# Two transformer blocks with 16 small heads: a head's stack in half of the partitions, restacked in three chunks, no clearing

## What is computed

```python
ada = silu(c) @ W_ada + b_ada            # six vectors of 144: shift, scale, gate, twice
h = layernorm(x) * (1 + scale) + shift
q, k, v = split(h @ W_qkv + b_qkv)       # 16 heads of 9 channels
p = softmax(q @ k.T / 3)                 # block 1: keys after the query are masked out
x = x + gate * ((p @ v) @ W_proj + b_proj)
h = layernorm(x) * (1 + scale2) + shift2
x = x + gate2 * (act(h @ W_fc1 + b_fc1) @ W_fc2 + b_fc2)
```

## Time and profile before

| | us |
|---|---|
| three runs, median (lowest to highest) | 379.49 (379.43 to 381.12) |
| profiled execution, first to last instruction | 382.2 |
| TensorE busy (2020 matmul instructions) | 305.8 |
| VectorE busy | 260.8 |
| ScalarE busy | 195.1 |
| POOL busy | 72.8 |

### The profile page before, as it was taken

The page is one execution under the profiler, slowest core; times in us unless marked ns, Lnnn a source line. Parts: engine busy times, 40 slices in busy tenths (PEclk is TensorE's granted clock), DMA queues, the critical chain, the costliest instruction groups (busy, mean ns, idle before and its releaser), DMA issues.

```text
span 382.2 us, 5927 instructions
## 1 busy us (share of the span) xinstructions
PE 305.8 (80%) x2020; PEld 165.7 (43%) x2020; DVE 260.8 (68%) x575; ACT 195.1 (51%) x414; POOL 72.8 (19%) x157
## 2 busy tenths in 40 slices
PE   2044399697999999889993879999953999999567
PEld 2023282122334363445341545565431565647366
DVE  6999589674858798996851667879633668831363
ACT  4037310274573755894781127745613456894352
POOL 5934500010102615501100010110100011010000
PEclk9999585588989999999997968999968799999969
DMA  6402645420000000000044100000451000000000
GB/s 173 116 0 79 143 92 157 103 72 17 1 2 2 0 4 1 2 1 3 1 121 100 60 7 0 3 1 13 128 96 53 3 1 3 3 1 17 16 2 31
DMA packets 11285, 15.57 MB, mean 41 GB/s; under 512 B 1774, under 2 KB 9909, under 8 KB 10824
## 3 DMA queue, kind: packets, MB, share of 16 engines
q1 hardware_dynamic: 10744, 15.00, 14.9%
q0 software_dynamic: 512, 0.20, 0.2%
HBM read 10.67 MB, written 4.13 MB: 39 GB/s over the span
## 4 chain that ended last, share of the span: by engine, by line
PE 53%; DVE 17%; DMA 14%; issue 6%; ACT 5%; SPq 4%; POOL 1%; DVEq 0%; ACTq 0%; POOLq 0%
PE PB L1147 11%; PE OB L1167 10%; DMA KS<-qk_parts 10%; PE PB L1129 9%; PE PB L1209 5%; DVE hn L968 4%; DMA QS<-mT 3%; SPq L668 3%; DVE negm L1014 3%; PE PB L1104 3%; DVE parts L998 2%; DVE rest L995 2%; PE PB L1174 2%; PE PB L1064 2%; PE PB L1150 1%
## 5 line engine op out<-in xcount | busy, mean ns | idle before, releaser
L1014 DVE TENSOR_REDUCE negm<-PB 128x1 f32<-128x512 f32 (+3 forms) x256 | 136.3, 583 | 62.4 <-PE PB L1131 39.2
L841 ACT ACTIVATE probs<-PB 128x512 f32<-128x512 f32 (+3 forms) x256 | 116.4, 521 | 80.2 <-PE PB L1150 47.0
L1129 PE MATMUL PB<-KS,QS 96*128 96x512 bf16 (+3 forms) x256 | 87.2, 387 | 21.1 <-DMA KS<-qk_parts 20.3
L1147 PE MATMUL PB<-QS,KS 96*128 96x512 bf16 (+3 forms) x256 | 81.4, 360 | 8.5 <-DMA QS<-mT 6.9
L1167 PE MATMUL OB<-probs,V 128*10 128x512 f32 (+3 forms) x512 | 59.7, 538 | 0.9 <-ACT probs L841 0.6
L1129 PEld LDWEIGHTS PB<-KS,QS 96*128 96x128 bf16 x256 | 26.2, 105 | 65.5 <-issue 42.0
L1147 PEld LDWEIGHTS PB<-QS,KS 96*128 96x128 bf16 x256 | 25.0, 101 | 52.9 <-issue 34.1
L768 POOL CAST msp<-negm 128x16 bf16<-128x16 f32 x16 | 4.3, 266 | 161.6 <-DVE negm L1014 161.6
L1104 PE MATMUL PB<-ident,hn 128*16 128x128 f32 (+1 forms) x64 | 12.1, 336 | 22.7 <-DVE hn L968 22.7
L1131 PE MATMUL PB<-mask_qk,identb 128*128 128x128 bf16 x128 | 29.4, 244 | 0.0
L1150 PE MATMUL PB<-mask_kq,identb 128*128 128x128 bf16 x128 | 27.0, 226 | 0.0
(11 more groups left out here) (135 smaller groups left out, 453.6 us busy)
## 6 DMA issues: line engine op xcount, KB each, us to landing
qk_parts<-parts SPq DMA_DIRECT2D x8, 384.0 KB, 2.5
QS<-qk_parts SPq DMA_DIRECT2D x4, 324.0 KB
KS<-qk_parts SPq DMA_DIRECT2D x4, 324.0 KB
QS<-qk_parts SPq DMA_DIRECT2D x8, 108.0 KB
KS<-qk_parts SPq DMA_DIRECT2D x8, 108.0 KB
QS<-qk_parts SPq DMA_DIRECT2D x4, 216.0 KB
KS<-qk_parts SPq DMA_DIRECT2D x4, 216.0 KB
X<-in_x SPq DMA_DIRECT2D x2, 288.0 KB, 3.2
```

The costliest lines, as they stand in the source:

```text
L841: nc.scalar.activation(probs[:, kt % 2, j, q0:T], bank_of(item)[:, q0:T], ACT.Exp, scale=SCALE).then_inc(bank_free[BANK[item]], 1)
L1014: nc.vector.tensor_reduce(negm[:, g % 2, qt, j:j + 1], bank[:, 0:keys_of(g // (B * NG), qt)], AX.X, ALU.max, negate=True).then_inc(bank_fr ...
L1129: ins = nc.tensor.matmul(o[:, 0:w], q, KS[b][0:KROWS, h + j, 0:w], start=True, stop=(l == 0))
L1147: ins = nc.tensor.matmul(bank[:, q0:T], KS[b][0:KROWS, h + j, kt * P:(kt + 1) * P], QS[b][0:KROWS, h + j, q0:T], start=True, stop=(l == 0))
```

## The change

- A head's stack takes 57 rows (KROWS = MROW + 3) and no cleared rows. Even heads lie at partitions 0 to 56, odd heads at 64 to 120; `QS` and `KS` are 128 x 8 x 512. Products of an even and of an odd head thus use different row tiles of TensorE.
- Units of a group run tile by tile with the four heads inside (`UNITS`), so parity alternates. In block 1 the two masks of a pair are issued together behind its second product.
- `qk` is cut in three chunks of heads (0 to 6, 7 to 13, 14 and 15), each with its queries and keys. SP writes each chunk's six slots to DRAM with six DMAs and reads them back with four (queries and keys, even and odd heads). Each chunk has its semaphores. The memsets and the copy that cleared stacks are gone; ones are sent once per batch and parity.
- `hT`: the last 16 channels are modulated on VectorE before the transpose (`hr`, five operations), stacked there, transposed as 96 columns. The fp32r split of the first 128 channels is gone: `qk` and `fc1` are one float32 product over 128 channels and one fp32r product of 96 rows. `wsplit` shrinks to stacking the last rows.
- `acol` computes the modulation of the last 16 channels for all partitions (wide products). `proj`'s residual product has 17 rows.
- Block 1's MLP: ScalarE writes tanh only, VectorE's gate reads x from the bank; the factors 0.5 are moved to the gate weights.
- Batch 0's x and the first qkv weights are loaded on ScalarE's queue. The maxima's parts go by two DMAs of POOL instead of one. Weights no longer share memory with MLP buffers.
- The planner has new costs and priorities (HASTE for batch 0's head 2000 instead of 20000, HOLD for shift 1 instead of 2).

```diff
-KROWS = 96
+CHUNKS = [(0, 7), (7, 14), (14, H)]
+STRIP = P // 2
+SLOTS = 6
+MROW = SLOTS * D
+KROWS = MROW + 3
...
+UNITS = [(t, j) for t in range(NT) for j in range(HG)]
...
+        def strip(h, n):
+            return slice(STRIP * (h % 2), STRIP * (h % 2) + n)
...
+                if kind == "parts":
+                    sp.wait_ge(parts_ready, QKN[("qk", l, b, i)])
+                    n = width(i) // 2
+                    for w, runs in enumerate((((0, 3, 1, 0), (0, 2, 1, 3), (0, 1, 1, 5)),
+                                              ((0, 1, 3, 0), (1, 1, 2, 3), (2, 1, 1, 5)))):
+                        for s, many, times, slot in runs:
+                            src = parts[w * n:(w + 1) * n, i, s:s + many, :]
+                            if times > 1:
+                                src = src.to_broadcast([n, times, T])
+                            dst = scratch[l][b][i][w, slot:slot + many * times].rearrange("s d h t -> (d h) s t")
+                            sp.dma_start(dst, src).then_inc(parts_out[i], 16)
+                    continue
                 if kind == "qk":
+                    if l and i == 0:
+                        full(sp, ("scores", (b + 1) * NG - 1, LAST))
+                    sp.wait_ge(parts_out[i], 6 * 16 * (l * B + b + 1))
+                    h0, h1 = CHUNKS[i]
+                    for q in range(2):
+                        first = h0 + (h0 + q) % 2
+                        rows, many = slice(STRIP * q, STRIP * q + MROW), len(range(first, h1, 2))
+                        for w, dst in enumerate((QS[b], KS[b])):
+                            src = scratch[l][b][i][w].rearrange("s d h t -> (s d) h t")[:, first - h0:h1 - h0:2, :]
+                            sp.dma_start(dst[rows, first // 2:first // 2 + many, :], src).then_inc(stacked[l * B + b][i], 16)
...
-                        nc.gpsimd.memset(KS[0][0:KROWS, :, :].bitcast(U32), 0).then_inc(k_zeroed[0], 1)
-                        nc.gpsimd.memset(QS[0][0:KROWS, :, :].bitcast(U32), 0).then_inc(q_zeroed[0], 1)
-                        nc.gpsimd.memset(KS[1][0:KROWS, :, :].bitcast(U32), 0).then_inc(k_zeroed[1], 1)
...
+                elif kind == "hr":
+                    link(nc.vector.tensor_tensor(y, hn[:, t0:t1, P:C], row_of(SC), ALU.mult))
+                    link(nc.vector.tensor_tensor(y, y, row_of(SH), ALU.add))
...
+                    nc.vector.tensor_copy(hs[:, t0:t1, 65:65 + R], y)
+                    link(nc.vector.tensor_copy(hs[:, t0:t1, 1:1 + R], y))
+                    nc.vector.tensor_tensor(hs[:, t0:t1, 33:33 + R], y, hs[:, t0:t1, 1:1 + R].bitcast(F32),
+                                            ALU.subtract).then_inc(hr_ready, 1)
...
                 elif kind == "qk":
...
-                    wide_product(bank, w_qk[l], w_qkv_s[l], c * P, QKW[c], 0).then_inc(filled_bank, 1)
+                    nc.tensor.matmul(bank[0:w, :], w_qk[l][:, cols], hT[:, :], start=True, stop=False)
+                    nc.tensor.matmul(bank[0:w, :], w_s[l][:, cols], hT_s[:, :], start=False, stop=True).then_inc(filled_bank, 1)
...
+                    rows, i = strip(h + j, MROW), (h + j) // 2
+                    ins = nc.tensor.matmul(bank[:, 0:w], QS[b][rows, i, qt * P:(qt + 1) * P], KS[b][rows, i, 0:w],
+                                           start=True, stop=(l == 0))
+                    if l == 0:
+                        ins.then_inc(filled_bank, 1)
+                    elif u % 2:
+                        for x in (u - 1, u):
+                            ins = nc.tensor.matmul(bank_of(("max", g, x))[:, w - P:w], identb[:, :], mask_qk[:, :],
+                                                   start=False, stop=True)
+                            ins.then_inc(bank_full[BANK[("max", g, x)]], 1)
...
-                        ins = nc.tensor.matmul(o, aT_r[:, tok], g_proj_r[l][b][:, :], start=False, stop=True)
+                        ins = nc.tensor.matmul(o, aT_r[0:R + 1, tok], g_proj_r[l][b][:, :], start=False, stop=True)
```

More of the change, by code:

```diff
@@ L119, with width, column, chunks_of @@
 BANKS = 7
+UNITS = [(t, j) for t in range(NT) for j in range(HG)]
+LAST = len(UNITS) - 1
+def width(c):
+    return 2 * D * (CHUNKS[c][1] - CHUNKS[c][0])
+def column(c):
+    return 2 * D * CHUNKS[c][0]
+def chunks_of(g):
+    h0, h1 = g % NG * HG, g % NG * HG + HG
+    return [c for c, (a, z) in enumerate(CHUNKS) if a < h1 and h0 < z]
+def layer(g):
+    return g // (B * NG)
 def keys_of(l, qt):
@@ L129, in first_query, with freed_by @@
     return kt * P if l else 0
+def freed_by(item):
+    kind = item[0]
+    if kind in ("hT", "aT", "mT", "scores") or kind == "fc1" and item[1] == 0:
+        return "ACT", item
+    return "DVE", ("gate", *item[1:]) if kind == "fc1" else item
 def steps():
@@ L177, in steps @@
             if norm and norm != item[:4]:
-                after += [("PE", ("hT", *norm[1:], r, 0)) for r in range(2)]
-            norm = item[:4]
+                after += [("PE", ("hT", *norm[1:], 0, 0))]
             add("side", "DVE", item, 1060 * size, *after)
+        elif kind == "hr":
+            after = [("DVE", ("acol", l, rest[1]))]
+            if norm and norm != ("norm", *item[1:4]):
+                after += [("PE", ("hT", *norm[1:], 1, 0))]
+            norm = ("norm", *item[1:4])
+            add("side", "DVE", item, 900, *after)
@@ L203, in steps @@
+            add("side", "PE", item, 1100 * size, *(("ACT", ("hT", l, b, 1, r, rest[-1])) for r in range(2)), ("POOL", ("fcs", l)))
+            add("side", "ACT", item, (430 * size + 90) * (1 if l else 2), ("PE", item), *mlp)
             if l == 0:
-                add("side", "DVE", item, 620 * size, ("ACT", item))
-        elif kind == "tanh" and l == 0:
-            add("side", "ACT", item, 520 * size, ("DVE", ("fc1", *item[1:])))
+                add("side", "DVE", item, 540 * size + 80, ("ACT", item))
+        elif kind == "tanh":
+            add("side", "ACT", item, 430 * size + 90, ("DVE", ("fc1", *item[1:])))
@@ L268, in plan @@
             if not isinstance(follow, int):
-                behind.setdefault(("POOL", follow[1]) if follow[0] == "rows" else follow, []).append((engine, item))
+                behind.setdefault(follow, []).append((engine, item))
         queue.append(item)
@@ L300, in plan @@
                 item = queues[q][at[q]]
-                ends = []
-                for follow in after[engine, item]:
-                    if isinstance(follow, int):
-                        ends.append(follow)
-                    elif follow[0] == "rows":
-                        ends.append(done.get(("POOL", follow[1]), inf) + 2000 + HANDOVER)
-                    else:
-                        ends.append(done.get(follow, inf) + HANDOVER)
-                start = max([free[engine], *ends])
+                start = max([free[engine], *(f if isinstance(f, int) else done.get(f, inf) + HANDOVER for f in after[engine, item])])
                 if start == inf:
@@ L347, in plan @@
             holder[k] = (item, stream)
-    return order, bank, before
-ORDER, BANK, BEFORE = plan()
+    return order, bank, before, max(done.values())
+ORDER, BANK, BEFORE, PLANNED = plan()
 def ordinals(kinds):
```

780 lines of the change are left out of this document (360 added, 420 removed).

## The result

The kernel after takes **415.08 us** (median of 5 runs, 411.73 to 425.44), the kernel before, beside it on the same chip, 381.12 (379.43 to 383.38). The ratio is 1.0929, 95% interval 1.0838 to 1.102: slower by 34 us. 356 us had been forecast. The profiled execution has a span of 409.9 us against 382.2.

The account below looks back on a forecast made before the run. TensorE was taken as the bound in layer 0's attention, with a slow start and two stack-transfer holes. Terms -18 - 12 - 21 + 14 + 8 + 6 + 3 - 3 = -23 gave 359 of span, forecast 356 us, range 332 to 375.

Parts of the forecast that it names:

- VectorE and ScalarE: Start and tail: smaller hT split and a ScalarE copy gone from layer 1's MLP, -3 us (bounds 0, -8).
- Start, -18: Before the first scores: memsets gone, faster loads and stack transfers, first scores near 51 us; -18 us (bounds 12 and 24).
- 0, no row prices it: Planner's rewritten order of items: no effect on time, 0, with 5 us either way.
- Layer 1's holes, -12: TensorE's two waits for layer 1's stacks: about 5 of each 10.8 us stay; -12 us (bounds 0 and 20).
- Layer 0's row tiles, -21: Layer 0's 256 maxima and score products: neighbours of opposite parity overlap, 38% off; -21 us (bounds 0 and -27.6).
- Layer 1's row tiles, +14: Layer 1's 128 pairs: changes of tile form around whole-array masks outweigh overlap; +14 us (bounds +8, +31).
- Side work +8: Products between attention's (qk, v, transposes, fc1, fc2, weights): some 70 runs meet form changes; +8 us (bounds 0 and 20).
- projection and gates +6: Projection's residual product, from 96 rows to 17: its 16 pairs of products cost more; +6 us (bounds +2, +7).
- float32 +3: Float32 products in place of three fp32r ones: slower at full width, faster at half; +3 us (bounds -2, +6).
- some 5 us on one block: Start: the wide modulation's 12 small products on a cold TensorE, some 5 us.
- Rival (a): Every maximum and score: row tiles don't overlap (partner issued too late, or hardware serializes); 394 us, chance 0.06.

Follow-up runs that it names:

- all_mends: Kernel after with half-array masks in layer 1, pairs kept adjacent, merged modulation products, and planner figures putting the first group's maxima first; 390.38 us, ratio 1.03.
- lean: Kernel after with layer 1's masks as 64-row halves in row tiles, pairs kept adjacent, and one modulation product of 32 columns for two; 387.71 us, ratio 1.024.
- one_tile: Kernel after with even and odd heads both reading the stacks' lower half, so no products overlap (attention not the reference's); 483.27 us, ratio 1.262.
- full_rows: Kernel after with attention's products one at a time over all 128 rows of the stacks (attention not the reference's); 400.24 us, ratio 1.0478.

## Why the prediction was wrong, step by step

It forecast TensorE +10 us (-21 + 14 + 8 + 6 + 3) and 33 us less waiting (start, holes, VectorE and ScalarE). Measured: +37 and -10. Of the 27 us that TensorE's sum was off, the modulation blocks are 15.4, layer 0's tiles 9.5, side work, projection, gates and float32 products 3.2 and the weighted sums 3.1, less 3.9 in layer 1's tiles. Most of the other 23 us are the start.

- **Start, -18: the step that failed, in two ways.** The first maxima came at 38.4 us where 32 were forecast. The normalization took 3.24 us (at 13.18) and not 1.14; POOL's work for the MLP's weight stack ran beside it, which may be why, but no run takes it away. And SP had chunk 0's parts to issue from 24.45 us, not 20; the six DMAs then took 2.72 us where I put 3.4. More was lost after that: the first scores were forecast for 51 us and came at 72.7. Between the first group's maxima stood a modulation block (6.4 us), the second batch's head and POOL's weight stacks, ahead of the split of the maxima on POOL's queue, which began at 65.25 us. I had called the order "0, no row prices it". But mending that isn't enough: all_mends reaches 50.08 us and ends no earlier than lean. The assumption beneath, that an earlier start comes through, is what failed. TensorE's total work from there on sets the end: what is pushed out of the start is done later (8.0 us), and more of the work meets the lower clock (20 us more of it at 1.2 GHz than in lean).
- **Layer 1's holes, -12: right.** TensorE's idle gaps before the first maxima of the two batches were 6.2 + 3.2 and 4.3 + 6.5 us, and are 4.4 and 5.4 now: 20.3 us in all, and 9.8.
- **Layer 0's row tiles, -21: right mechanism, size off.** Neighbours of opposite parity overlap almost wholly, but the saving was 11.5 us, not 21. The overlaps are nearly as many as I had counted: 84 of layer 0's 256 products start within 0.03 us of the next (2 before), and 84 times 0.216 is 18 us. Only 26 of the 128 pairs are adjacent in the planned order; most of the other overlaps are with some other product of the other parity. What ate the rest is longer intervals behind other products, waits and changes of form: at full clock 21 of them are over 0.47 us, with 12.7 us in all, where before has 9 with 5.5. With all 128 pairs adjacent 100 products overlap, 29 intervals are over 0.47 us (17.2 us), and the saving is 15.2 (72.8 to 57.6). The term had no such share.
- **Layer 1's row tiles, +14: right**, +10.1 measured. The change of form was costed about right (0.43 us for a pair of 256 columns and its masks, where 0.49 was put for 320); that it could be avoided wasn't seen, and it was worth 13.6 us. The Trainium skill (TensorEngine Tiling, "Key Properties") says that changing the mode drains the engine; the trace agrees, with 0.21 us from a pair of 256 columns to its mask (350.46 to 350.67), for products that need 0.11 at full clock.
- **Side work +8, projection and gates +6, float32 +3: right together**, 17 forecast, 20.2 measured (123.0 - 104.4 and 8.3 - 6.7). By kind: qk and fc1 +4.5, the projection +4.9, v +2.5; the rest is transposes, fc2 and gates. The size is in part luck: this work spends 10 us more at 1.2 GHz than before (27.9 against 17.7), up to 5 us by the estimate above, and the prediction had no term for that.
- **The modulation blocks: a missing term.** I put some 5 us on one block, in the start. There are four: +15.4 us of TensorE, of which the merged form gives 7.8 back and 9 us of the time.
- **The weighted sums: a missing term**, +3.1. It is no separate cause if the clock's part is as estimated: 13.5 us of them are at 1.2 GHz where 5.2 were before.
- **The clock: a missing term.** The prediction held TensorE's clock fixed. From the first scores on TensorE worked 38 us more at 1.2 GHz, at most 19 of its 37 us by the estimate above. That the clock can depend on how attention's products use the array is shown by one_tile against full_rows. Why it falls where it does in the kernel after isn't shown, nor is any run the kernel after with its clock alone changed.

Rival (a) named the right side and its first reason, partners issued apart; but its condition, under 40% of the overlap counted, wasn't met (11.5 of 21 is 55%), and its price, 394, was too low too. The loss is accounted for by the mends: 13.6 (changes of form at the masks), 9.3 (modulation) and 8.4 (split pairs) are 31 one by one and 27.4 together, in lean. The 8.5 us that lean still lies above before have no experiment of their own: its attention products take 26.5 us less of TensorE than before's, projections, MLP and transposes 21.3 more, modulation blocks 8.5 more, the weighted sums and gates 3.9 more. From the first scores on it works 65 us at 1.2 GHz where before works 41, which by the estimate above is up to 12 us, and at full clock its work would be that of before (256 and 257 us). So the lower clock alone could be what is left. Undoing the float32 products or the 17-row projection alone wasn't tried.

## What to carry to other kernels

A product of 57 rows in a row tile is only cheap if its partner runs beside it and nothing over the whole array stands between the pairs: order the pairs in the plan, and give masks the tiles' form too. Before filling in a forecast for a kernel that TensorE bounds, count every instruction that the change adds to it, many small products with weights of their own above all (here they cost by the product, not by the column). A gain ahead of such a stretch, in the start, doesn't come through by itself. And look at the granted clock before and after: here work was saved and in part paid back by a lower one.

## What the runs showed of the hardware that was not expected

- At the same count, widths and order of attention's products, the granted clock was 0.74 with 54 and 57 rows in one row tile, one at a time, and 0.89 with 128 rows over the whole array. In time, 483 against 400 us.
- Less work for TensorE went with a lower clock: without the maxima's masks lean's time at 1.2 GHz rose from 113 to 126 us and the time stayed (387.7 and 387.9), and in the kernel before it rose from 80 to 91 us. The granted clocks of the timed runs agree: 0.84 against lean's 0.85 to 0.86, and 0.89 against 0.90.
- In a stretch in which TensorE was busy 27.5 of 27.5 us (118 to 145.5) its clock was 0.57; in it are small products with 16 columns, weighted sums and pairs.
- A float32 product over 128 rows took 0.57 us for its two passes with 32 columns and 0.54 with 16, both at the slow pace.
